# Routed expert products with the weights stationary, and the first shared group prepared inside the last attention step

## What is computed

```python
x = L0_attn_x                                  # (2, 2048, 512)
xn = layernorm(x)
x = x + attention(xn, ...) + ffn(xn, ...)

def ffn(x):                                    # 4096 tokens of 512
    probs = softmax(x @ w_gate)                # 8 experts
    combine = top2(probs), normalized to sum 1
    gu = einsum('th,ehf->etf', x, w_gate_up)   # (8, 512, 2*256)
    act = silu(gate) * up
    eo = einsum('eti,eih->eth', act, w_down)   # (8, 256, 512)
    routed = einsum('te,eth->th', combine, eo)
    shared = silu_and_mul(x @ w_sh_gate_up) @ w_sh_down   # (512, 2*1024), (1024, 512)
    return routed + shared
```

## Time and profile before

| | |
|---|---|
| median of 3 runs | 1273.26 us (1271.31 to 1275.28) |
| the profiled execution, its own time | 1275.16 us |
| its span, first to last instruction | 1273.4 us |
| PE busy | 1205.0 us, 95% of the span |
| PEld, DVE, ACT, POOL busy | 64%, 52%, 37%, 39% |
| set-up, to about | 40 us |
| attention, to | 450 us |
| `shared(0)`, to | 713 us |
| `routed()`, to | 1018.6 us |
| `shared(1)`, to | 1273 us |

### The profile page before, as it was taken

One profiled execution on the slowest core, in us unless ns is written; L12 is line 12 of the kernel. 1 busy time (PEld: TensorE's weight loads), 2 busy tenths in 40 slices (PEclk: granted clock), 3 DMA queues, 4 the chain that ended last, 5 costly groups with the idle time before them and its releaser, 6 DMA issues. The chain is left out here.

```text
span 1273.4 us, 29250 instructions
## 1 busy us (share of the span) xinstructions
PE 1205.0 (95%) x10768; PEld 816.2 (64%) x10768; DVE 661.2 (52%) x1410; ACT 475.8 (37%) x1030; POOL 491.4 (39%) x432
## 2 busy tenths in 40 slices
PE   3899999999999779999999899999999899999997
PEld 3666677677677457777777444444444477777775
DVE  7878888998988578633333222222222123333333
ACT  6455555555555362322222233333333311111111
POOL 3446656665675200445401122222222044444444
PEclk9999999999999889999999999999999999999999
DMA  6589888788778655344323687888889334444444
GB/s 207 129 220 216 196 214 247 200 222 236 207 222 238 197 199 181 95 109 96 104 100 45 165 194 191 188 196 185 193 193 186 97 133 150 149 149 148 149 149 133
DMA packets 269373, 217.40 MB, mean 171 GB/s; under 512 B 196784, under 2 KB 203056, under 8 KB 269296
## 3 DMA queue, kind: packets, MB, share of 16 engines
q1 hardware_dynamic: 255344, 180.03, 53.3%
q0 software_dynamic: 12848, 35.47, 9.8%
q10 hardware_dynamic: 1104, 0.81, 0.2%
HBM read 115.97 MB, written 56.51 MB: 135 GB/s over the span
## 5 line engine op out<-in xcount | busy, mean ns | idle before, releaser
L1434 PE MATMUL sc<-xT,WG 128*128 128x256 f16 x3072 | 348.9, 274 | 11.6 <-DVE WD L1730 8.4
L1434 PEld LDWEIGHTS sc<-xT,WG 128*128 128x128 f16 x3072 | 302.0, 98 | 61.7 <-DVE WD L1730 8.9
L1445 PE MATMUL sc<-WG,raw 128*128 x852 | 208.4, 381 | 5.4 <-DMA raw<-raw 3.2
L1869 DVE SCALAR_TENSOR_TENSOR actv<-sc,up_inv,sg 128x512 f32<-128x512 f32 x64 | 48.0, 751 | 246.1 <-ACT sg L1706 245.9
L1415 POOL DMA_INDIRECT raw<-xs_dram,slots x71 | 67.3, 948 | 280.2 <-DMA raw<-raw 208.3
L1706 ACT ACTIVATE sg<-sc,gate_inv 128x512 f32<-128x512 f32 x64 | 43.9, 687 | 303.3 <-PE sc L1434 300.8
L1452 PE MATMUL yp<-WD,ah 128*128 128x512 f16 x512 | 152.3, 379 | 1.4 <-DVE al L1874 1.4
L1445 PEld LDWEIGHTS sc<-WG,raw 128*128 128x128 f16 x852 | 83.7, 98 | 91.8 <-issue 8.8
L1937 POOL DMA_INDIRECT raw<-y_dram,gidx x64 | 64.3, 1004 | 151.8 <-DVE ys L1850 101.5
L791 PE MATMUL ring<-hT,qkvT 128*128 128x256 f16 x1024 | 120.9, 275 | 2.0 <-PEq L213 2.0
L2074 DVE TENSOR_TENSOR alr<-rat,ahr 128x256 f16<-128x256 f32 x71 | 30.2, 425 | 159.3 <-ACT ahr L2051 159.3
(11 more groups left out here) (260 smaller groups left out, 1776.4 us busy)
## 6 DMA issues: line engine op xcount, KB each, us to landing
y_dram<-raw SPq DMA_DIRECT2D x71, 256.0 KB
xl<-in_L_attn_x SPq DMA_DIRECT2D x16, 512.0 KB, 4.2
wraw<-in_L_ffn_w_gate_up SPq DMA_DIRECT2D x16, 512.0 KB, 4.6
xs_dram<-xs SPq DMA_DIRECT2D x16, 512.0 KB, 3.7
xT_dram<-x SPq DMA_DIRECT2D x16, 512.0 KB, 2.6
xr<-in_L_attn_x SPq DMA_DIRECT2D x16, 512.0 KB, 5.4
x_dram<-x SPq DMA_DIRECT2D x32, 256.0 KB, 2.1
xT<-xT_dram SPq DMA_DIRECT2D x16, 512.0 KB, 5.4
```

Source lines behind the costliest of these rows:

```text
L1434: ins = pe.matmul(gu[:, h, f * tokens:(f + 1) * tokens].rearrange("p (u t) -> p u t", u=B), w[:, kk, b, a0:a0 + P], x[:, :, a * KT + kk, : ...
L1445: ins = pe.matmul(gu[bank], x(kk, a), w[:, 0, kk, b, :], start=(i == 0), stop=(i == len(done) - 1))
L1869: v.scalar_tensor_tensor(out=actv[:, g % 2], in0=gu[g % 2][:, 1].rearrange("p (f t) -> p f t", f=FT), scalar=up_inv[:, 1:2], in1=sg[:], op ...
```

## The change

`gate_up_rows` now takes four parts of 128 gate or up columns. In each the weights are stationary and the 128 tokens move: 48 matmuls of 128 columns instead of 12 of 512. The product then has the hidden columns on the partitions, as `down` wants them, so the two turns and their PSUM tiles go. The combine weight can no longer be a factor per partition there and moves to the result: `cw` holds all 71 tiles' weights, worked out once, and scales ACT's copy of the result. ACT now takes the high half of tile r ahead of the result of tile r-1. In the last routed tile the first product of `shared(1)` is cut in two: two parts before `down`, two after it.

`WG`, `WD` and `x16` now live from the start, and the attention's own buffers are laid into `WG` and `WD` (`lent`). The last attention step loads `x16`, makes the halves of group 0 (ACT after its step, DVE in `low_first` around the second `residual`), and PE issues the first shared product at the end of the attention block instead of at the start of `shared(0)`.

```diff
@@ build @@
+        WG = sb(kept, "WG", [P, GROUPS + EXPERTS, KT, 2, 2 * FFN], F16)
+        WD = sb(kept, "WD", [P, GROUPS + EXPERTS, FT, 2, DIM], F16)
+        x16 = sb(kept, "x16", [P, 2, B, 2 * KT, P], F16)
...
-        qkvT = sb(attn, "qkvT", [P, KT, QKV], F16)
+        qkvT = lent(attn, "qkvT", [P, KT, QKV], F16, (0,))
+        xn = lent(attn, "xn", [P, 2, B, DIM], F32, (1,))
...
@@ attention, SP @@
                 else:
                     for g in range(2):
                         load_group(sp, k, g)
+                    sp.wait_ge(S["logits_ready"], NCH)
+                    sp.wait_ge(xT_out[0], 16 * (NCH // 2))
+                    sp.dma_start(x16[:, 0], xT_dram[0]).then_inc(x_ins[0][0], 16)
@@ attention, PE @@
             run_steps(pe, prologue, step)
+            pe.wait_ge(split, KT)
+            pe.wait_ge(x_ins[0][0], 16)
+            gate_up(pe, sc[:, 0:2], x16[:, 0], WG[:, 0]).then_inc(gu_fulls[0], 1)
@@ attention, ACT @@
             run_steps(act, prologue, step)
+            act.wait_ge(S["wscale_ready"], 1)
...
+            for i in range(PIECES):
+                dst = WG[:, 0, i, 0, :] if i < KT else WD[:, 0, i - KT, 0, :]
+                act.activation(dst, raw[:, 0, i], ACT.Copy, scale=wscale[:, 2:3] if i < KT else wscale[:, 3:4]
+                               ).then_inc(high, 1)
@@ attention, DVE @@
+            def low_first(some):
+
+                v.wait_ge(S["wscale_ready"], 1)
+                for i in some:
+                    v.wait_ge(high, i + 1)
...
                 residual(0, q, par, st)
                 if has_norm:
                     h_low(q + 1, par)
+                if not front:
+                    low_first(range(KT))
                 residual(1, q, par, st)
+                if not front:
+                    low_first(range(KT, PIECES))
@@ experts @@
-        def gate_up_rows(pe, gu, bank, x, w, parts):
-
-            done = [(kk, a, b) for kk in range(KT) for a, b in PASSES]
-            for i in parts:
-                kk, a, b = done[i]
-                ins = pe.matmul(gu[bank], x(kk, a), w[:, 0, kk, b, :],
-                                start=(i == 0), stop=(i == len(done) - 1))
-            return ins
+        def gate_up_rows(pe, bank, x, w):
+
+            for part in range(2 * FT):
+                for kk in range(KT):
+                    for a, b in PASSES:
+                        ins = pe.matmul(bank[:, part * P:(part + 1) * P], w[:, 0, kk, b, part * P:(part + 1) * P],
+                                        x(kk, a), start=(kk == 0 and (a, b) == PASSES[0]),
+                                        stop=(kk == KT - 1 and (a, b) == PASSES[-1]))
+            return ins
@@ routed, PE @@
-                            gate_up_rows(pe, gu, 1 - par, slot_rows(r + 1), WG[:, nxt], FIRST)
-                        pe.wait_ge(S["act_ready"], r + 1)
-                        for f in range(FT):
-                            ins = pe.transpose(at[par][:, f, :], actv[:, par, f * P:(f + 1) * P], ident[:])
-                        ins.then_inc(S["at_full"], 1)
-                        if not last:
-                            gate_up_rows(pe, gu, 1 - par, slot_rows(r + 1), WG[:, nxt], REST).then_inc(S["gu_full"], 1)
+                            gate_up_rows(pe, gu[1 - par], slot_rows(r + 1), WG[:, nxt]).then_inc(S["gu_full"], 1)
                         else:
                             pe.wait_ge(x_ins[1][0], 16)
-                            gate_up(pe, gu_whole[0], xT[:, 0], WG[:, 0], B * P).then_inc(gu_fulls[1], 1)
+                            pe.wait_ge(S["act_ready"], r + 1)
+                            gate_up(pe, gu_whole[0], xT[:, 0], WG[:, 0], (0, 1))
...
                         down(pe, yp[par], (ah[:, par], al[:, par]), WD[:, own], True, True).then_inc(S["y_full"], 1)
+                        if last:
+                            gate_up(pe, gu_whole[0], xT[:, 0], WG[:, 0], (2, 3)).then_inc(gu_fulls[1], 1)
                         return after
@@ routed, ACT @@
+                    for r in range(SLOT_TILES):
+                        par = r % 2
+                        act.wait_ge(S["gu_full"], r + 1)
+                        act.activation(sg[:, par], gu[par][:, 0:FFN].rearrange("p (f t) -> p f t", f=FT), ACT.Silu,
+                                       scale=gate_inv[:, 0:1]).then_inc(S["sg_ready"], 1)
+                        act.wait_ge(S["act_ready"], r + 1)
+                        act.activation(ah[:, par], actv[:, par], ACT.Copy).then_inc(S["ah_ready"], 1)
+                        if r > 0:
+                            y_evac(r - 1)
@@ routed, DVE @@
+                    v.tensor_scalar(cw[:], slots[:].bitcast(F32)[:, 0:SLOT_TILES, 1], out_inv[:, 0:1], None, ALU.mult
+                                    ).then_inc(S["cw_ready"], 1)
...
-                        v.tensor_tensor(al[:, par], at[par][:], ah[:, par], ALU.subtract).then_inc(S["al_ready"], 1)
-                        v.wait_ge(S["act_ready"], r + 1)
-                        weight(q + 1, par)
+                        v.tensor_tensor(al[:, par], actv[:, par], ah[:, par], ALU.subtract).then_inc(S["al_ready"], 1)
```

More of the change, by code:

```diff
@@ L154, in build, with lent @@
         raw = sb(kept, "raw", [P, 2, PIECES, DIM])
+        GROUPS = w_sdn.shape[0] // FFN
+        WG = sb(kept, "WG", [P, GROUPS + EXPERTS, KT, 2, 2 * FFN], F16)
+        WD = sb(kept, "WD", [P, GROUPS + EXPERTS, FT, 2, DIM], F16)
+        x16 = sb(kept, "x16", [P, 2, B, 2 * KT, P], F16)
+        rooms = [WG[:].rearrange("p g k s c -> p (g k s c)"), WD[:].rearrange("p g k s c -> p (g k s c)")]
+        taken = [0, 0]
+        def lent(ctx, name, shape, dt=F32, among=(0, 1)):
+            halves = (4 if dt == F32 else 2) // 2
+            for d in shape[1:]:
+                halves *= d
+            for i in among:
+                if taken[i] + halves <= rooms[i].shape[1]:
+                    part = rooms[i][0:shape[0], taken[i]:taken[i] + halves]
+                    taken[i] += (halves + 15) // 16 * 16
+                    part = part if dt == F16 else part.bitcast(dt)
+                    dims = "abcdefg"[:len(shape) - 1]
+                    return part if len(dims) == 1 else part.rearrange(
+                        f"p ({' '.join(dims)}) -> p {' '.join(dims)}", **dict(zip(dims[1:], shape[2:])))
+            return sb(ctx, name, shape, dt)
+        x_ins = [[sem(kept, f"x_in{i}_{half}") for i in range(2)] for half in range(2)]
+        gu_fulls = [sem(kept, f"gu_full_{half}") for half in range(2)]
+        high = sem(kept, "high")
+        split = sem(kept, "split")
         raw_in = [sem(kept, f"raw_in{i}") for i in range(2)]
@@ L230, in build @@
[L230 to L241 removed]
+            mark = list(taken)
@@ L530, in load_group, with gate_up @@
     sp.dma_start(raw[:, KT:], k["sdn"][g]).then_inc(done, 16)
+def gate_up(pe, gu, x, w, parts=range(2 * FT)):
+    for part in parts:
+        h, f = part // FT, part % FT
+        for kk in range(KT):
+            for a, b in PASSES:
+                ins = pe.matmul(gu[:, h, f * 2 * P:(f + 1) * 2 * P].rearrange("p (u t) -> p u t", u=2),
+                                w[:, kk, b, part * P:(part + 1) * P], x[:, :, a * KT + kk, :],
+                                start=(kk == 0 and (a, b) == PASSES[0]),
+                                stop=(kk == KT - 1 and (a, b) == PASSES[-1]))
+    return ins
 def wait_apart(eng, sem, value, passed):
@@ L554, in attention @@
         k[x] for x in "wtop wall wexp wrec wscale esq gate_inv up_inv out_inv".split())
+    WG, WD, raw, raw_in, sc, x_ins, gu_fulls, high, split = (
+        k[x] for x in "WG WD raw raw_in sc x_ins gu_fulls high split".split())
     xn, xs, x16, hn, hs, hT, stats, mv, ve, sd, rstd, rve, hv, hv2, hsd, hT_in, xT_in, S = (
@@ L1360, in experts @@
     w_gu, w_dn, w_sgu, w_sdn, NCH, B = (k[x] for x in "w_gu w_dn w_sgu w_sdn NCH B".split())
-    GROUPS = w_sdn.shape[0] // FFN
+    GROUPS, WG, WD, xT, x_ins, gu_fulls, high, split = (
+        k[x] for x in "GROUPS WG WD x16 x_ins gu_fulls high split".split())
     HALF = NCH // 2
@@ L1397, in experts @@
         gu_half = [sc[:, 0], sc[:, 2]]
-        gu_fulls = [sem(c, f"gu_full_{half}") for half in range(2)]
         rows_full = sem(c, "rows_full")
@@ L1455, in down @@
             return ins
-        FIRST, REST = range(0, 6), range(6, 3 * KT)
         SENDS = 4
@@ L1579, in raw_routed @@
                         sp.sem_inc(raw_in[par], 16)
-                    load(0, 0)
+                    if half == 0:
+                        sp.dma_start(x1[:, 0], x1_steps[0]).then_inc(x1_in[0], 16)
+                    else:
+                        load(0, 0)
                     if half == 0:
```

207 lines of the change are left out of this document (89 added, 118 removed).

## The result

The changed kernel takes **1387.57 us** (median, 1386.14 to 1388.07) against 1273.26 us before: a ratio of **1.089** (95% interval 1.086 to 1.091). It is slower, as forecast, but above the range of 1333 to 1380 us. The profiled execution took 1388.07 us, 112.9 more than that of before.

The account below looks back on a forecast made before the run. The array bounds the kernel before; PE's sequencer, computing addresses, was to bound the routed tiles after. Terms 81.8 + 0.9 - 4.6 - 1 = +77.1 us on a median of 1273.26 gave 1350 us, range 1333 to 1380.

Parts of the forecast that it names:

- 69 tiles: Routed tiles: the period grows by 1.185 us from 4.175 us, over 69 tiles +81.8 us.
- first tile: First routed tile, array at half clock: 5.3 us of array where 4.2 us stood, given as +0.9 us.
- last tile, to the next block's product: Last routed tile: splitting the shared product 24 to 24 brings the last down product forward, -3.0 us.
- no half-clock start in the last block: Next block's first product: PE idle under 1 us beforehand, so full clock is expected, -1.6 us.
- all ahead of the routed product (end of attention -1, rest 0): End of attention: most PE idle time saved is paid again, -1 us, bounds -3 and +5; new buffer addresses 0.
- the last part of the prediction: Signs expected in the profile after: 32 register instructions per product, PE idle at "issue", clock 1.0, tiles 5.3 to 5.4 us.
- The DMA's 63%: Routed tiles: the DMA queues' busy share falls from 81% to about 63%.
- the sum of 5.36 us of sequencer per tile: Routed tile: 36 register instructions, 4.46 us, plus 0.9 us make 5.36 us of sequencer against 3.99 us of array.
- The fixed 0.9 us: PE's sequencer, each routed tile: expert's number 0.6 us, some 0.1 us after it, two waits of about 0.1 us.
- The pitch of 0.124 us for all 36: PE's sequencer, each routed tile: 36 register instructions follow each other every 0.124 us, 4.46 us in all.
- The array stays the bound: Rival, routed tiles: register instructions overlap and a tile takes the array's 3.99 us; stage gains 9 us, 1260 us; chance 0.08.
- The clock falls: Rival, routed tiles: idling drops the clock to 1.2 GHz, 1525 us in full, 1370 for a tenth; over 30 us, chance 0.06.

Follow-up runs that it names:

- e1: Changed kernel with the expert's place fixed by tile number in both routed products, so no register instruction stands in them; the number is still loaded: 1261.27 us.
- e2: Kernel before, tokens still stationary and turns kept, with its product cut into 48 matmuls of 128 columns and 32 register instructions: 1393.37 us.
- e3: Changed kernel without the third pass of the routed product: 32 matmuls instead of 48, still 32 register instructions: 1383.58 us.
- e8: Changed kernel with the load of the expert's number moved from behind the product to ahead of it, behind the last down product: 1369.87 us.
- e6: Kernel before with only the change's last tile (shared product split around the last down product) and new attention buffer addresses: 1269.02 us, ratio 0.9975.
- e5: Kernel before with only the change's end of attention, including the new buffer addresses; routed and last tile as before: 1271.11 us, ratio 0.9987.
- e9: Changed kernel, old end of attention; DVE copies only the high weight parts to fixed addresses, 20 register instructions per tile, load ahead of product: 1264.75 us, ratio 0.9941.
- e10: Changed kernel without its routed product: end of attention and last tile as in the change, routed tiles as before: 1266.27 us, ratio 0.9954.
- e7: Changed kernel, old end of attention; DVE copies the expert's whole gate_up slice to fixed addresses, so no register instructions in the product: 1278.46 us, ratio 1.0032.
- e4: Changed kernel with the expert's number read for the first two tiles only; the builder then also kept most computed addresses: 1261.58 us.

## Why the prediction was right and where it was wrong

By its own terms, the two profiled executions side by side. The stage begins with tile 0's product at 706.73 (709.88 before); from there to tile 0's down product are 10.44 us (9.18 before), in which the first tile lies:

| term | forecast | measured |
|---|---|---|
| 69 tiles | +81.8 | +119.7 |
| first tile | +0.9 | +1.3 |
| last tile, to the next block's product | -3.0 | -2.9 |
| no half-clock start in the last block | -1.6 | -2.1 |
| all ahead of the routed product (end of attention -1, rest 0) | -1 | -3.15 |
| sum (of unrounded terms) | +77.1 | +112.9 |

**The mechanism was right.** The sequencer, not the array, became the bound: 32 `FUSED_REGOPS` per product, PE's idle time at "issue", clock 1.00, as the last part of the prediction asked for. (The DMA's 63% also came out as forecast, but by luck: it was worked out for a tile of 5.36 us, and for 5.91 the same sum gives 57%.) e1 removes them and gets the array's 4.0 us; e2 adds them to the old orientation and gets 5.9; e3 takes away matmuls and gets nothing.

**The step that failed is the sum of 5.36 us of sequencer per tile**, which is 5.91; 0.55 us times 69 is 38 us, the whole miss. In the changed kernel's trace the load, its arithmetic and its check take 0.92 us (forecast 0.7), from there to the product's first register instruction are 0.75 (4 x 0.124 and two waits of 0.1, 0.70), and the product takes 4.21 (3.97): together 5.88. Two terms were too small:

- *The fixed 0.9 us.* "From 854.7 to 855.3, 0.6 us, some 0.1 us before what follows it": the instruction was timed where it stood in the kernel before, with the load itself at 303 ns. Behind the long product it takes 0.3 to 0.9 us (488 above), in the mean 0.25 more of the sequencer. Shown by e8: behind the down product the price is the old one and 18 us come back.
- *The pitch of 0.124 us for all 36.* The pitch itself was right to the nanosecond, in every trace with long chains. But in a chain it is broken: after every eighth register instruction comes a pause, about 60 ns more in the mean (in the tile above at 904.0, 905.0, 906.0 and 907.1). 32 of them took 4.21 us where 32 x 0.124 = 3.97. The earlier trace rows showed four in a row, from which no such pause could be seen. It comes by the count of register instructions, with 32 matmuls between them as with 48 (e3), and with either operand stationary (e2). Its cause was not tried.

The range was too narrow for that reason: it allowed 7 us for the fixed part and 13 for the pitch, errors of reading, and took it that an instruction costs the same in another place and in a longer chain. For the load it is the place that counts and not whether the sequencer has slack: in e1 it has slack and the load costs 0.66 us behind the long product, in e8 it has none and the load costs 0.38 behind the down product.

**The other terms.** The first tile's own sum has a slip: 5.3 us of array where 4.2 stood is +1.1, not +0.9; +1.3 was measured, in one trace each. The last tile came out within 0.1 us. The table's -2.1 is all that changed behind the next block's first product; that product itself took 1.57 us less, as forecast. Together the two are -5.0, and -4.9 over all traces (e6), where -4.6 was forecast. For the end of attention, nearly each step went as worked out: the second `residual` 3.3 us behind the first where it was 1.85, the block opening late because PE had to be empty (the later of the two ways named), the second product after a pause and mostly at half clock. But the second product ended 27.1 us after the scales (436.58 to 463.71) where it ended 25.3 us after them before (442.06 to 467.38): +1.8 us, where the prediction's 464 to 468 against 467.4 is -3.4 to +0.6. So this end saved nothing by itself in this trace, and that the row lies within the forecast's bounds is luck: of the measured -3.15 us, -5.5 lie ahead of attention's last `wtop` transpose (434.08 against 439.56), where executions differ by more than that anyway, and +2.3 behind it, which over more executions shrinks to +0.3 (e5's table).

**The rivals.** *The array stays the bound*: wrong at 0.124 us, as the trace had said; e9 shows it true at 20 register instructions per tile. The 9 us that this rival gave the stage did not come, though, with 20 or with none: e1's mean tile is 4.14 us against 4.17, 2.5 us over 69 tiles, and e5 and e10 have 4.13 with the old product. *The clock falls*: wrong for this kernel, but not by much of a margin. PE stood idle for 15% of the 370 us above, in gaps of at most 1.2 us, and the granted clock was 1.00. The Trainium skill, "TensorE: Matmul & The Clock Gate", section "A second HAM failure mode: psum-queue depth-cycling", would have had it swing between both levels under brief idling between groups of matmuls; the changed kernel's trace does not agree. e3's does: with a third of the product's matmuls left out and gaps of at most 1.4 us the clock swung between both levels, 0.91 in the mean. It cost nothing there, as the array was not the bound.

## What to carry to other kernels

Count the instructions that compute addresses before making matmuls smaller. An engine's sequencer has its own budget: here 36 addresses at 0.124 us, and 1.4 us for the expert's number, waits and pauses, made a tile of 5.9 us out of 4.0 us of matmuls, and the profile of before showed it only in the sequencer's rows, not in any busy share. If data-dependent addresses are too many, move part of the data to fixed places with an engine that has time (e9), and put loads of registers behind short work (e8). And look at the mean of a stage, not at its usual tile: the array's 0.1 us per tile never reached the time.

## What was not expected of the hardware

- A load of a register on PE's sequencer costs 0.38 us behind six matmuls of 512 columns and 0.63 us behind a long chain of weight loads, matmuls and register instructions (e8 against the changed kernel). In e1, where no register instruction stands in the product, it was 0.66: so it is not they that lengthen it, but something in the long row of matmuls or weight loads; a third fewer of them (e3) leave it at 0.65. The cause was not tried.
- A pause of about 60 ns in the mean after every eighth register instruction of a chain (124 ns pitch otherwise).
- DVE's copy of 128 x 4096 halves per tile lengthened GpSimd's gathers from 947 to 1263 ns; half the copy gave 993. The DMA queues' busy share, 78% to 82% in most runs, was 94% with the copy (e7), but 91% in e4 over the same stretch (730 to 1000 us) without one.
- With 32 instead of 48 matmuls between the same register instructions the granted clock fell from 1.00 to 0.91 in 730 to 960 us, in stretches of 3.4 us (e3), with gaps of PE hardly longer than in the changed kernel (1.4 against 1.2 us).
